# Sums over the embedding dimensions in two pieces with a 17th column, and twenty more idle-time matmuls, in a cross-interaction tower

## The reference

```python
x0 = xk = stack of the 39 gathered embedding rows           # (b, 39, 16)
for idx, (W, b) in enumerate([(w0, b0), (w1, b1), (w2, b2)]):
    z = relu(einsum('bhd,bkd,hks->bsd', x0, xk, W) + b[None, :, None])
    if idx != 2:
        xk = z[:, :64, :]; direct.append(z[:, 64:, :])
    else:
        direct.append(z)
z = sum(concatenate(direct, axis=1), axis=-1)               # (b, 64 + 64 + 128)
h = relu(concatenate([z, dense_ctx], 1) @ W_top1 + b_top1)  # 272 -> 512
h = relu(h @ W_top2 + b_top2)                               # 512 -> 256
y = h @ W_top3                                              # 256 -> 1
```

## Time and profile before

| what | value |
|---|---|
| time, median of 3 runs | 1295.45 us (1294.12 to 1296.54) |
| profiled execution | 1292.88 us, its span 1290.7 us |
| TensorE matmul busy | 1230.8 us, 95% |
| VectorE busy | 1090.5 us, 84% |
| GpSimd busy | 909.0 us, 70% |
| ScalarE busy | 664.3 us, 51% |
| mean granted TensorE clock | 0.991 |
| DMA | 233.55 MB, mean 181 GB/s |

### The profile page before, as it was taken

The page is one execution under the profiler, slowest core; times in us unless marked ns, Lnnn a source line. Parts: engine busy times, 40 slices in busy tenths (PEclk is TensorE's granted clock), DMA queues, the critical chain, the costliest instruction groups (busy, mean ns, idle before and its releaser), DMA issues.

```text
span 1290.7 us, 15168 instructions
## 1 busy us (share of the span) xinstructions
PE 1230.8 (95%) x4038; PEld 761.3 (59%) x4038; DVE 1090.5 (84%) x967; ACT 664.3 (51%) x708; POOL 909.0 (70%) x581
## 2 busy tenths in 40 slices
PE   0489999999999999999999999999999999999998
PEld 0336566666656666666656666666666666666652
DVE  1258988988999988988999888989999988989850
ACT  1135654556555555556555555556655555555532
POOL 6678778787878787787878787787878755555520
PEclk9879999999999999999999999999999999999999
DMA  7199888888998888888987888888988877888500
GB/s 191 31 221 211 193 189 197 193 201 199 216 199 181 189 188 193 199 200 199 220 191 181 189 191 195 191 201 205 220 185 180 189 196 186 194 200 203 132 1 0
DMA packets 134531, 233.55 MB, mean 181 GB/s; under 512 B 16434, under 2 KB 23715, under 8 KB 134401
## 3 DMA queue, kind: packets, MB, share of 16 engines
q1 hardware_dynamic: 83053, 151.03, 50.7%
q10 hardware_dynamic: 41474, 79.71, 24.2%
q0 software_dynamic: 9984, 2.58, 2.3%
HBM read 229.39 MB, written 6.23 MB: 183 GB/s over the span
## 4 chain that ended last, share of the span: by engine, by line
PE 82%; DVE 6%; issue 5%; POOL 4%; DMA 2%; ACT 1%; DVEq 0%; ACTq 0%; POOLq 0%
PE z_odd L844 36%; PE z_even L844 29%; PE z_even L877 8%; PE z_odd L877 4%; DVE whole L734 3%; POOL gathered L484 3%; PE whole_psum L871 1%; DVE whole_psum L734 1%; DVE rest L741 1%; DMA x_rep<-x_rows 1%; PE x_odd L871 1%; PE x_even L897 1%; PE x_even L871 1%; PE x_odd L897 1%; POOL rest L497 1%
## 5 line engine op out<-in xcount | busy, mean ns | idle before, releaser
L497 POOL TENSOR_TENSOR rest<-whole,head 128x1024 fp32r<-128x1024 f32 x256 | 610.2, 2395 | 250.6 <-ACT head L608 247.7
L734 DVE TENSOR_TENSOR whole<-x_banks,x_rep 128x1024 f32<-128x1024 f32 x480 | 567.0, 1212 | 70.9 <-ACT x_banks L566 69.3
L608 ACT CAST head<-whole 128x1024 fp32r<-128x1024 f32 x256 | 268.7, 1050 | 189.8 <-DVE whole L734 134.4
L484 POOL DMA_INDIRECT gathered<-in_tbl,idx x312 | 296.8, 951 | 84.5 <-issue 76.9
L608 ACT CAST head<-whole_psum 128x1024 fp32r<-128x1024 f32 x160 | 162.2, 1014 | 121.8 <-DVE whole_psum L734 116.0
L844 PE MATMUL z_odd<-whole,w_whole 128*128 128x512 f32 x468 | 218.5, 595 | 2.8 <-DVE whole L734 2.8
L734 DVE TENSOR_TENSOR whole_psum<-x_banks,x_rep 128x1024 f32<-128x1024 f32 x160 | 196.1, 1225 | 13.5 <-DMA x_rep<-x_rows 12.0
L741 DVE TENSOR_TENSOR rest<-whole_psum,head 128x1024 fp32r<-128x1024 f32 x160 | 194.6, 1216 | 9.1 <-ACT head L608 8.9
L844 PE MATMUL z_even<-whole,w_whole 128*128 128x512 f32 x428 | 198.5, 592 | 0.0
L844 PE MATMUL z_odd<-head,w_rest 128*128 128x512 f32 x393 | 188.4, 480 | 1.1 <-POOL rest L497 0.6
L844 PE MATMUL z_even<-head,w_rest 128*128 128x512 f32 x375 | 175.2, 467 | 4.4 <-DVE rest L741 4.2
(11 more groups left out here) (90 smaller groups left out, 930.4 us busy)
## 6 DMA issues: line engine op xcount, KB each, us to landing
x_rep<-x_rows SPq DMA_DIRECT2D x128, 512.0 KB, 10.8
x_rep<-x_rows ACTq DMA_DIRECT2D x128, 512.0 KB, 11.8
x_shift<-x_rows SPq DMA_DIRECT2D x93, 546.0 KB
x_rep<-x_rows SPq DMA_DIRECT2D x32, 384.0 KB
x_rep<-x_rows ACTq DMA_DIRECT2D x32, 384.0 KB
x_rep<-x_rows SPq DMA_DIRECT2D x32, 256.0 KB
gathered<-in_tbl,idx POOLq DMA_INDIRECT x312, 7.5
x_rows<-xt_and_ctx SPq DMA_DIRECT2D x32, 78.0 KB
```

Source lines behind the costliest of these rows:

```text
L484: nc.gpsimd.indirect_dma_start(gathered[:, f, :], None, tables[f], bass.IndirectOffsetOnAxis(ap=idx[:, f:f + 1], axis=0)).then_inc(s_gathe ...
L497: nc.gpsimd.tensor_tensor(rest[:, split_slot(product)], whole_slot(product), head[:, split_slot(product)].bitcast(F32), ALU.subtract).then ...
L608: nc.scalar.copy(head[:, split_slot(product)], src).then_inc(s_head, 1)
L734: nc.vector.tensor_tensor(out[0:rows, 0:width, :], xk[0:rows, :].unsqueeze(1).to_broadcast([rows, width, N]), x0, ALU.mult).then_inc(s_pro ...
```

## The change

`direct01` and `direct2` get a 17th column. The sum of each becomes two reductions, all of them placed between layer 0's products and the wait for `x2_bank`: in a block's third tile (t % 4 = 2) VectorE sums the 8 dimensions of the first two tiles of `direct2` into column 16; in the fourth (t % 4 = 3) the 12 dimensions of the first three tiles of `direct01` into its column 16; in the next block's first tile (t % 4 = 0) it sums the remaining dimensions and that column, 5 columns of `direct01` and 9 of `direct2`, into `sum01` and `sum2`. The reduction inside layer 2 is gone. ScalarE waits for the partial sum ahead of a block's first tile, and for the previous block's final sum ahead of the first tile that the partial sum does not cover. `WARM_UP` goes from 24 to 34, and 10 such matmuls more follow layer 0's last pair in step -1.

```diff
 TRANSPOSES_AFTER = 1
-ADD_01_AFTER = 7
+TILES_IN_PART_01 = 3
+TILES_IN_PART_2 = 2
...
-TOGETHER = TPB
...
-WARM_UP = 24
+WARM_UP = 34
+FILL_UP = 10
...
-        direct01 = sb("direct01", [P, P, DIM])
-        direct2 = sb("direct2", [P, P, DIM])
+        direct01 = sb("direct01", [P, P, DIM + 1])
+        direct2 = sb("direct2", [P, P, DIM + 1])
...
             def out_layer2(t):
                 act.wait_ge(s_used, before(t, 2, PAIRS))
-                if t.first % TOGETHER == 0:
-                    wait(act, s_sum2, t.visits(TOGETHER))
+                if t.first % TPB == 0:
+                    wait(act, s_part2, t.blocks())
+                elif t.first % TPB == TILES_IN_PART_2:
+                    wait(act, s_sum2, t.blocks())
...
+            def wait_direct01(t):
+
+                if t.first % TPB == 0:
+                    wait(act, s_part01, t.blocks())
+                elif t.first % TPB == TILES_IN_PART_01:
+                    wait(act, s_sum01, t.blocks())
...
-            def add_dims(out, direct, t, done):
+            def add_tiles(direct, tiles, done):
+
+                nc.vector.tensor_reduce(direct[:, :, DIM], direct[:, :, 0:tiles * DPT], AX_X, ALU.add).then_inc(done, 1)
+
+            def add_rest(out, direct, tiles, t, part, done):
 
                 b = t.blocks()
                 cols = out[:, b * P:(b + 1) * P] if t.turn is None else out[:, bass.ds(b * P, P)]
-                nc.vector.tensor_reduce(cols, direct[:], AX_X, ALU.add).then_inc(done, 1)
-
-            def add_layer2(t):
+                dve.wait_ge(part, t.blocks(1, 1))
+                nc.vector.tensor_reduce(cols, direct[:, :, tiles * DPT:], AX_X, ALU.add).then_inc(done, 1)
+
+            def add_rest_of_block(t):
+
+                dve.wait_ge(s_d01, t.count(2, 2))
+                add_rest(sum01, direct01, TILES_IN_PART_01, t, s_part01, s_sum01)
                 dve.wait_ge(s_d2, t.count(1, 1))
-                add_dims(sum2, direct2, t, s_sum2)
-
-            def add_layers01(t):
-                dve.wait_ge(s_d01, t.count(2, 2))
-                add_dims(sum01, direct01, t, s_sum01)
+                add_rest(sum2, direct2, TILES_IN_PART_2, t, s_part2, s_sum2)
+
+            def add_in_gap(t):
+
+                last = t.plus(-1)
+                if t.first % TPB == 0 and (t.turn is not None or t.first > 0):
+                    add_rest_of_block(last)
+                if t.first % TPB == TILES_IN_PART_2:
+                    dve.wait_ge(s_d2, last.count(1, 1))
+                    add_tiles(direct2, TILES_IN_PART_2, s_part2)
+                if t.first % TPB == TILES_IN_PART_01:
+                    dve.wait_ge(s_d01, last.count(2, 2))
+                    add_tiles(direct01, TILES_IN_PART_01, s_part01)
...
                 if has_layers12(t):
-                    if t.first % TOGETHER == 0 and (t.turn is not None or t.first > 0):
-                        add_layer2(t.plus(-1))
+                    add_in_gap(t)
                     dve.wait_ge(s_x2, t.count(2, 2))
-                    ends = t.first % TOGETHER == TOGETHER - 1
-                    layer12(t, 2, x2_bank, {ADD_01_AFTER: lambda: add_layers01(t)} if ends else {})
+                    layer12(t, 2, x2_bank)
...
-            add_layer2(Tile(TILES - 1))
+            add_rest_of_block(Tile(TILES - 1))
...
-            for n in range(WARM_UP):
-                nc.tensor.matmul(z[1][:], w_head[:, n % (N // UNITS), :],
-                                 w_head[:, 0:N // UNITS, :].rearrange("p c s -> p (c s)"), start=True, stop=True)
+            def keep_busy(count):
+
+                for n in range(count):
+                    nc.tensor.matmul(z[1][:], w_head[:, n % (N // UNITS), :],
+                                     w_head[:, 0:N // UNITS, :].rearrange("p c s -> p (c s)"), start=True, stop=True)
+
+            keep_busy(WARM_UP)
...
                     for j in range(PAIRS0):
                         layer0(t, j)
                         if not has_layers12(t) and j + 2 < PAIRS0:
                             select(j + 2)
+                    if not has_layers12(t):
+                        keep_busy(FILL_UP)
```

More of the change, by code:

```diff
@@ L230, in build_kernel @@
         s_d2 = sem("direct2_ready")
+        s_part01 = sem("three_tiles_of_01_added")
+        s_part2 = sem("two_tiles_of_2_added")
         s_sum01 = sem("sum01_ready")
@@ L635, in out_layer1 @@
                 relu(x2_bank[HALF:P, :], zz[0:HALF, :], bias[0:HALF, 1:2]).then_inc(s_x2, 1)
-                if t.first % TOGETHER == 0:
-                    wait(act, s_sum01, t.visits(TOGETHER))
+                wait_direct01(t)
                 relu_by_sample(direct01[HALF:P], t, zz[HALF:P, :], bias[HALF:P, 1:2]).then_inc(s_d01, 1)
@@ L647, in next_direct @@
                 nxt = t.plus(1)
-                if nxt.first % TOGETHER == 0:
-                    wait(act, s_sum01, nxt.visits(TOGETHER))
+                wait_direct01(nxt)
                 relu_by_sample(direct01[0:HALF], nxt, z_of(t, 0)[HALF:P, :], bias[HALF:P, 0:1]).then_inc(s_d01, 1)
@@ L743, in rest_of, with layer12 @@
                                         ALU.subtract).then_inc(s_rest_v, 1)
-            def layer12(t, layer, xk, between):
+            def layer12(t, layer, xk):
                 later = []
@@ L754, in layer12 @@
                         later.append(j)
-                    if j in between:
-                        between[j]()
                     while later and (later[0] <= j - DEFER or j == PAIRS - 1 or
@@ L777, in body @@
                     dve.wait_ge(s_x1, t.count(2, 2))
-                    layer12(t, 1, x1_bank, {})
+                    layer12(t, 1, x1_bank)
                 if has_layer0(t):
@@ L856, in mlp_job @@
                     if m == 0:
-                        pe.wait_ge(s_sum01, TILES // TOGETHER * (half + 1) // (B // N))
-                        pe.wait_ge(s_sum2, TILES // TOGETHER * (half + 1) // (B // N))
+                        pe.wait_ge(s_sum01, TILES // TPB * (half + 1) // (B // N))
+                        pe.wait_ge(s_sum2, TILES // TPB * (half + 1) // (B // N))
                 elif layer == 2:
```

## The result

The changed kernel takes 1285.81 us (median of 4 runs, 1285.40 to 1287.14) beside 1295.25 for the kernel before: the ratio is 0.9929, 95% interval 0.9914 to 0.9945, or 9.4 us less. Measured again later it gave 0.9932 (0.9919 to 0.9946), 1285.84 us beside 1294.81. The forecast was 1286.8 us.

The account below looks back on a forecast made before the run. TensorE, busy 95% of the span, was taken to bound the kernel. Gains of 7.7 us (stalls) and 0.9 (start), 8.6 in all, from the 1295.45 us median gave 1286.8 us, range 1283.5 to 1290.5.

Parts of the forecast that it names:

- The seven stalls: Blocks 0 to 6, fourth tile: the reduction inside layer 2 delays TensorE 1.10 us each; removing it gains 7.7 us.
- The four reductions: VectorE's sums per block: 1.74, 1.21, 1.34 and 0.81 us, 5.10 in all in place of 4.55.
- rival 3: Reductions read 17-element rows slower than assumed; at three times the time, 21 us slower, 1316 us; chance 0.04.
- The holes: VectorE idles 2.62 us between layer 0's products and x2; the pieces leave 1.4, 0.9 and 0.5 us.
- x2 idle time gone in the first tile of a block: Sign of a wrong forecast: VectorE no longer waits for x2 there, where 0.5 us was to be left.
- The second reserve: VectorE's lead over TensorE, about 1.2 us, read in layer 2, covering the pieces behind layer 0 beyond the hole.
- rival 1: The stall moves to late x_rep loads or a small hole; half the gain returned gives 1290.7 us; chance 0.10.
- The start, 0.9 us: Ahead of steady state: faster clock and earlier store gain 0.9 us, bounded by a 3.1 loss and a 5 gain.
- Layer 2 starts no more than 0.81 us sooner: Tile 0: VectorE waits for x_shift, so layer 2 gains at most 0.81 us plus what the store gains.
- The ten have no part: The ten matmuls behind layer 0 gain nothing, since TensorE waits at 87.70 for VectorE's rest at either clock.
- Rival 2: The start's clock gain does reach the end, 5 us, giving 1282.8 us; chance 0.09.
- Rival 4: Despite the added matmuls the clock falls, only later; start gives 0 to 1 us, 1287.7 to 1286.7; within forecast's 0.76.

Follow-up runs that it names:

- the doubled sums: The changed kernel with each reduction reading its elements twice: 1293.98 us, ratio 0.9994 to the kernel before.
- the sums alone: The changed kernel with the sums in pieces but 24 early matmuls and none behind layer 0: 1287.85 us, ratio 0.9942 to the kernel before.

## Why the prediction was right, step by step

- **The seven stalls, 7.7 us.** Right: 7.5 us in the steady time (1152.4 less 1144.9), 1.07 a block for the 1.10 read off the chain. The period of 144.6 was met.
- **Outside the span, in no term.** About 0.4 us was gained there (1.8 us instead of 2.2). The prediction had not asked for it, and its cause is open.
- **The four reductions, 5.10 us.** Right to 0.01 us each: 1.74, 1.21, 1.34, 0.81. The one rate held for rows of 17 elements. So the rule on SBUF lines, of the Trainium skill's page "SBUF — State Buffer", section "Door 1: The DMA port swizzle", does not carry over to these reductions: the measurement decides, and rival 3 has no ground left. The stepped relu moved by 0.02 us, within its bounds.
- **The holes, 2.62 us.** Right for the fourth tile (0.95 left of it against 0.9), not for the first: 0.5 was to be left, and in tile 8 the two sums outgrow the hole by 0.28 us, while in the others up to 0.63 is left. "x2 idle time gone in the first tile of a block" was named as a sign of being wrong. It came in two of the seven blocks of the profile and cost nothing, because the lead covers it.
- **The second reserve, "VectorE's lead of about 1.2 us".** Wrong where it was used. The 1.17 was read behind product 7 of layer 2 and holds there (the partial sum put back cost 0.55 us). At the start of layer 2, where the pieces stand, it is 0.75, as the doubled sums showed. Rival 3's reckoning had the hole of the first tile too large as well (2.62 for at most 2.3). At twice the time it expected the first tile to lose 0.5 a block, and it lost 0.83 to 1.49: the balance tips at twice the time of the reductions, where the ratio was 0.9994, and not at 2.3 times. The sum of the forecast was not touched, since the 0.28 us by which a piece outgrew its hole is well within either lead.
- **New waits at nothing.** Right: none shows. Of rival 1's mechanism a little does: VectorE waits 16.5 us in all for `x_rep`, where it was 13.4, and one tile of the profile is 0.23 us late.
- **The early matmuls hidden.** Right: 0.75 us to spare.
- **The start, 0.9 us.** Direction and bounds right, the size not settled. What the steady time and the 0.4 us outside the span leave is 1.5 us in the first measurement (9.4 in all) and 1.1 in the second (9.0); the change against the sums alone is 2.0. Without the 0.4, which the forecast did not have, the two totals would be 9.0 and 8.6 beside its 8.6. The mechanism, the store behind x_rep, was seen (13.10 us to landing), but it was only half of it: with the store moved away x_shift lands no earlier, while the DMA engines are full (share 1.02). By "DMA: Bandwidth & Descriptors", section "Queues, rings and completion order", of the Trainium skill the store starts behind the loads. The trace agrees (2.00 us to landing when issued at 78.56, 13.10 when issued at 70.35), though engines that are merely full would look the same.
- **"Layer 2 starts no more than 0.81 us sooner".** The bound held and was beside the point: in the profile after it started 3 us later. The profile of before was an early execution, 2.4 us under the median of its kind, and a start read from it is no mean. The profile after was a late one, 1.3 us over its median. The fairer pair is 106.47 for the sums alone and 104.77 for the changed kernel beside them: 1.7 us sooner, with x_shift awaited until 100.77, not 97 to 98. Why the shared transfers vary by such amounts from run to run stays open.
- **The ten have no part.** Not decided: 1286.79 without them, 1285.84 with them, in different sets and on different chips, intervals overlapping.
- **Rival 2, the clock's gain reaching the end.** The clock was full for the whole of layer 0, and some 8 us of TensorE's time there became 1.1 to 2 at the end. Rival 4, the clock falling all the same, did not happen in the profiled execution, but in five of the seven later profiles with the same early matmuls it did, for 3 us or more. So the 34 matmuls do not hold the clock reliably, and that the full clock is what gives the start its 1 to 2 us is likely but not shown.

## What to carry to other kernels

Work on an engine that is not the bound costs nothing in the holes where it waits for the bounding engine, and costs all that exceeds its lead anywhere else; measure the lead at the very place where the work is to stand, since it was 0.75 us at the start of a layer and 1.2 further on in it. The hole, too, is to be measured in the tile that is to be filled. Ahead of the steady state, ask which resource the chain hands over to: 8 us of faster matmuls were worth 1 to 2, because the next thing needed was a transfer. And split a time at the first tile of the steady state: that part agreed to 0.2 us between profiled executions whose totals differed by 28.

## What was not expected of the hardware

- VectorE sums rows of 17 float32 (68 bytes apart) at the rate of rows of 16: 5 columns in 0.81 us, 12 dimensions in 1.74.
- The granted clock stayed at 1.00 through the 39-row selects and layer 0 (57 to 84 us) in three profiles; in five others it fell to half on the way, and in one of those it stayed at half until 84. Entered at half, it stayed at half (0.50) from 57 to 76 us in the profile of before, although TensorE was busy for all of these 19 us.
- A store of 40 KB took 13.10 us to land behind the loads in its queue, and 2.00 us when it was issued later. Moving the stores ahead of the loads did not change when the data behind it arrived.
- One chip paused engines for up to 30 us ahead of tile 0 in one set (29.36 us in one profile) and did not in a later one.
